# Edge rows fetched by strip and half a ring at a time, instead of by third of a group

## What is computed

```
xn = layernorm(x)
m  = xn[src] @ Wg[:256] + edge_attr @ Wg[256:]          # 106250 edges
g  = segment_sum(m * deg^-0.5[dst], dst) + h_bias
a  = gelu((q @ (LN(k)^T LN(v) / N) + xn) @ w1 + b1) @ w2 + b2 + xn    # linear attention, 8 heads
x  = x + g + a
x  = x + layernorm(top-2 experts FFN(layernorm(x)) + layernorm(x))    # one routing for all rows
```

## Time and profile before

| | before |
|---|---|
| median of 3 runs | 1550.7 us |
| profiled execution | 1550.73 us |
| its span | 1548.9 us |
| edge phase (first to last matmul of L849) | about 64 to 1141 us |
| GpSimd: gathers of L527, busy | 814.9 us of 831 gathers |
| TensorE busy (share of the span) | 1126.2 us (73%) |
| DMA queue 1 (SyncE) | 149305 packets, 159.30 MB |
| DMA queue 0 (GpSimd) | 39888 packets, 108.97 MB |

### The profile page before, as it was taken

One profiled execution on the slowest core, in us unless ns is written; L12 is line 12 of the kernel. 1 busy time (PEld: TensorE's weight loads), 2 busy tenths in 40 slices (PEclk: granted clock), 3 DMA queues, 4 the chain that ended last, 5 costly groups with the idle time before them and its releaser, 6 DMA issues. The chain is left out here.

```text
span 1548.9 us, 22938 instructions
## 1 busy us (share of the span) xinstructions
PE 1126.2 (73%) x7317; PEld 815.4 (53%) x7317; DVE 682.0 (44%) x1616; ACT 485.8 (31%) x1006; POOL 977.3 (63%) x1005
## 2 busy tenths in 40 slices
PE   0167787877677777777677677667566499999997
PEld 0035454544444544444454444444333199999997
DVE  6144555455545553232222222231017656666665
ACT  5411111111111110221111112111027667767764
POOL 5577777777777777777777776767734224333332
PEclk9998888888878887788778878878779889999998
DMA  9976767776767675978888887889634100000001
GB/s 271 292 247 209 232 202 224 217 233 194 218 207 226 208 215 182 250 219 244 237 236 242 247 227 223 242 242 302 189 86 127 47 20 23 20 23 23 20 22 32
DMA packets 195653, 275.73 MB, mean 178 GB/s; under 512 B 20021, under 2 KB 166577, under 8 KB 194318
## 3 DMA queue, kind: packets, MB, share of 16 engines
q1 hardware_dynamic: 149305, 159.30, 35.0%
q0 software_dynamic: 39888, 108.97, 23.6%
q10 hardware_dynamic: 6375, 6.40, 1.2%
HBM read 255.38 MB, written 19.23 MB: 177 GB/s over the span
## 5 line engine op out<-in xcount | busy, mean ns | idle before, releaser
L527 POOL DMA_INDIRECT ring<-xn_table,src_sb x831 | 814.9, 981 | 281.0 <-issue 245.4
L849 PE MATMUL bank<-ring,s 128*32 128x512 f32 x1662 | 267.7, 725 | 282.0 <-DMA ring<-xn_table,src_sb 225.4
L863 PE MATMUL bank<-fl_t,wg 128*128 128x128 f32 x1120 | 221.0, 379 | 19.0 <-ACT fl_t L600 18.9
L849 PEld LDWEIGHTS bank<-ring,s 128*32 128x32 f32 x1662 | 39.8, 116 | 352.4 <-issue 272.7
L863 PEld LDWEIGHTS bank<-fl_t,wg 128*128 128x128 f32 x1120 | 211.9, 291 | 20.7 <-ACT fl_t L600 20.7
L1200 DVE TENSOR_TENSOR acc<-acc,bank 128x96 f32 x277 | 70.6, 255 | 342.5 <-PE bank L863 225.5
L1205 DVE TENSOR_TENSOR xt_lo<-bank,xt_hi 128x250 fp32r<-128x250 f32 (+1 forms) x75 | 37.8, 505 | 260.2 <-ACT xt_hi L600 260.2
L589 POOL TENSOR_TENSOR rx<-vex,half 125x2 f32<-125x2 f32 x25 | 17.7, 708 | 181.9 <-DVE nmx L1451 181.9
L1068 PE MATMUL bank<-xf_hi,fw_hi 128*128 128x256 f32 x400 | 113.5, 284 | 9.4 <-DVE fw_lo L1477 7.2
L1430 DVE TENSOR_TENSOR h_lo<-h,h_hi 128x512 fp32r<-128x512 f32 x100 | 95.8, 968 | 49.6 <-ACT h_hi L600 49.6
L1079 PE MATMUL bank<-fw_hi,h_hi 128*125 128x256 f32 x400 | 113.7, 284 | 0.0
(11 more groups left out here) (207 smaller groups left out, 2155.4 us busy)
## 6 DMA issues: line engine op xcount, KB each, us to landing
ring<-edges SPq DMA_DIRECT2D x207, 512.0 KB
ring<-xn_table,src_sb POOLq DMA_INDIRECT x831, 3.9
xnr<-xn_table SPq DMA_DIRECT2D x50, 125.0 KB
xnr<-xn_table SPq DMA_DIRECT2D x25, 250.0 KB
xch<-x SPq DMA_DIRECT2D x25, 250.0 KB
base_rows<-xch ACTq DMA_DIRECT2D x25, 250.0 KB
out<-res SPq DMA_DIRECT2D x25, 250.0 KB
acc<-x SPq DMA_DIRECT2D x5, 1120.0 KB
```

Source lines behind the costliest of these rows:

```text
L527: pool.indirect_dma_start(out=to, out_offset=None, in_=table, in_offset=bass.IndirectOffsetOnAxis(ap=index, axis=0),).then_inc(done, 16)
L849: mm = pe.matmul(ps_seg[t % 2][j * W:(j + 1) * W, :], lhsT=s32[:, t % 3, j * TS + i, :].bitcast(F32), rhs=ring[:, u, j, :], start=i == 0, ...
L863: mm = pe.matmul(ps_y[:, o * P:(o + 1) * P], lhsT=wg[:, c, o * P:(o + 1) * P], rhs=fl_t[:, c, :], start=c == 0, stop=c == 3)
```

## The change

`edge_load` now takes a group t instead of a third. It fetches strip by strip: for strip j one DMA reads, per partition, three consecutive rows (3 KB in one piece in DRAM) and writes them to three ring slots, the half of the ring that the group uses (slots 0 to 2 for even t, 3 to 5 for odd t). A group has four DMAs of 384 KB instead of three of 512 KB. Only two semaphores count them, one per half, and TensorE waits once per group, in its first third, for all four. SyncE issues the loads of group t+1 in its third 3t, ahead of that third's other loads, and waits before them until group t-1 is done, which is third 3t - 1 (`s_seg` at 3t).

```diff
-        def loaded(q):
-
-            return 16 * (q // RS + 1)
+        def loaded(t):
+
+            return 16 * ST * (t // 2 + 1) if t < NG - 1 else 16 * ST * (t // 2) + 16 * TS
...
-            def edge_load(q):
-
-                t, i = divmod(q, TS)
-                u = q % RS
-                wait_past(sp, s_seg, q - RS + 1)
+            def edge_load(t):
+
+                wait_past(sp, s_seg, TS * (t - 1))
+                u = TS * (t % 2)
                 if t < NG - 1:
-                    rows = edges[t * GE:(t + 1) * GE, :].rearrange("(j p k) d -> p j k d", p=P, k=TS)[:, :, i, :]
-                    sp.dma_start(ring[:, u, :, D:2 * D], rows).then_inc(s_e[u], 16)
+                    for j in range(ST):
+                        a = (t * ST + j) * SE
+                        rows = edges[a:a + SE, :].rearrange("(p k) d -> p k d", k=TS)
+                        sp.dma_start(ring[:, u:u + TS, j, D:2 * D], rows).then_inc(s_e[t % 2], 16)
                 else:
-                    rows = edges[FULL + i:E:TS, :]
-                    sp.dma_start(ring[0:rows.shape[0], u, 0, D:2 * D], rows).then_inc(s_e[u], 16)
+                    for k in range(TS):
+                        rows = edges[FULL + k:E:TS, :]
+                        sp.dma_start(ring[0:rows.shape[0], u + k, 0, D:2 * D], rows).then_inc(s_e[t % 2], 16)
...
-            for q in range(3):
-                edge_load(q)
+            edge_load(0)
...
             for q in range(NQ):
-                if q >= 3:
-                    edge_load(q)
+                if q % TS == 0 and q // TS + 1 < NG:
+                    edge_load(q // TS + 1)
                 if kv_at(q, 0) is not None:
                     kv_load(kv_at(q, 0))
...
-                pe.wait_ge(s_e[u], loaded(q))
+                if i == 0:
+                    pe.wait_ge(s_e[t % 2], loaded(t))
                 pe.wait_ge(s_gat[u], arrived(q))
```

## The result

The changed kernel takes 1810.81 us (median of 4 runs, 1787 to 1818), the kernel before 1550.45 in the same comparison. The ratio is 1.1623, 95% interval 1.1509 to 1.1738: slower by 16%. Ratio and interval leave out one of the four runs (1817.69 us), which is counted as one in a slower state. The profiled execution took 1808.09 us, its span 1806.2, 257.3 more than before. The forecast of 1743 had the sign and the closed loop; it was 68 us short.

What follows compares the result with a forecast made beforehand. GpSimd's gathers were taken to bound the edge phase, except the mix stretch, where TensorE also waits for SyncE's queue. 1550.7 us plus 176 for the mix stretch and 17 for the kv stretch gave 1743.7, stated as 1743, range 1625 to 1850.

Steps and rivals of the forecast that it cites:

- What bounds the kernel now: Edge phase: GpSimd's gathers, 15.4 us a group; in the mix stretch a 16.67 us period with TensorE waiting for SyncE's queue.
- Fewer or larger transfers: Edge loads: 207 pieces of 512 KB become 276 of 384 KB, with 3 KB runs in DRAM; priced at nothing.
- The order moved: SyncE's queue: mix load issued late behind 1536 KB; mix period 23.7 us against 16.67, 176 us over 25 groups.
- T: Mix stretch: time from the end of strip sums 3t-1 until the mix load has landed, put at 14.7 us.
- The first two parts: Terms of T: 1.7 us fixed, plus 7.1 us for 1536 KB of edge rows at 222 GB/s.
- the third part: Term of T: the 500 KB mix load, 4.0 us alone, 5.9 us beside the gathers.
- the harder rival: Mix and kv stretches both at their long bounds, ACT's store sharing engines with the burst: up to 1946 us; chance 0.07.
- The prediction's other estimate: Mix stretch: five engines at 27 GiB/s less gathers, 9.0 us for edge and mix rows; T = 10.7, 75 us more.
- The kv stretch: 34 groups in 17 pairs: late kv loads make a pair 30.4 us against GpSimd's 30.7; 17 us for jitter.
- The rival that loads overtake the pieces: Queue: mix load overtakes edge pieces or lands by 7.7 us, so no difference, 1551 us; chance 0.04.
- the faster one: Mix stretch: 3 KB pieces help, mix load not held up, GpSimd's 15.4 us binds; 32 us less, 1519; chance 0.07.
- The milder rival: Mix load goes at the edge pieces' pace: T = 11.1, period 20.1 us, 85 us more, 1636; chance 0.22.

Runs made afterwards that it cites:

- e1: Changed kernel with each group's kv loads and mix load issued ahead of the next group's edge pieces; 1697.88 us beside 1682.37, ratio 1.0090.
- e2: Kernel before, pieces still by third, but issued at the change's place and behind its wait; 1910.79 us beside 1682.37, ratio 1.1353.
- e9: Changed kernel with ACT's store issued two thirds later, behind the mix transposes; ratio to the kernel before 1.1279.
- e8: Changed kernel with mix loads and ACT's store each cut into partitions 0 to 111 and 112 to 124; ratio to the kernel before 1.0985.
- e3: Changed kernel with each mix load cut into partitions 0 to 111 and 112 to 124; ratio to the kernel before 1.1243.
- c_after: Changed kernel run again without edits, as reference on a chip of the experiments; 1941.96 us beside 1681.69, ratio 1.1554.
- e6: Changed kernel with two of four strip pieces ahead of the mix load and two behind, in the mix stretch alone; 1903.35 us, ratio to the kernel before 1.1314.
- e7: Changed kernel with the mix load behind the same wait but ahead of all four edge pieces; 1845.41 us, ratio to the kernel before 1.0984.
- e11: Changed kernel with mix load behind the same wait, ahead of edge pieces and cut at partition 112, ACT's store two thirds later; 1741.17 us beside 1694.43, ratio 1.0287.

## Why the prediction was right, and which term was too small

What bounds the kernel now, right: with the loads ahead (e1) the kernel is back within 0.9%, so the edge pieces themselves were no bound.

Fewer or larger transfers cost nothing, right in the mix stretch, by e1 and e2; in the kv stretch e2 leaves 20 us open between the shape and the wait for the whole group, where the loads come late. The packets show that 3 KB runs weren't even moved as longer ones. The rule that the prediction cites there is on whole transfers; that it would favour 3 KB pieces inside one was my reading of it.

The order moved, right: a closed loop from `s_seg` over SyncE's wait, the burst and the mix load to TensorE, 25 times. The part beside T, 9.0 us, measured 8.8 in the period shown.

T was the term that was mis-sized: 17.5 in the period shown (17.4 by the mean period less 8.8), not 14.7. The first two parts held as far as can be told: the last edge piece is issued near 914.3, and if it lands after the median of 6.3 us the pieces are in by 920.6, 8.8 us after the clock's start, as 1.7 + 7.1; no row shows this landing itself. Then the third part, the mix load, took the remaining 8.7 us where I had 5.9. I had scaled the lone store's time by 327/222, for the gathers. Two things were left out. One: ACT's store of 250 KB starts within 0.2 us of the edge burst; I had put it in the harder rival and not in the sum, and e9 and e8 price it at 1.2 and 1.5 us of wait. Two: the full engines don't move the 327 GB/s of the slice that I picked, but 241 to 365 from slice to slice. In e8 nearly everything is spread over all engines, and the edge pieces, mix load, store and eight gathers, 3.39 MB in 12.4 us, still average 273 GB/s. And one sign was misread: the share of 0.59 at 858 to 860 says nothing of the mix load issued at 858.79, for ahead of that issue, from 856 to 858, it is 0.56. That the load uses few engines is shown only by the tail after the change and by e3.

The prediction's other estimate, T = 10.7, was worked out from the 27 GiB/s an engine that the Trainium skill gives, page "DMA: Bandwidth & Descriptors", section "Specifications". It fell farther short of the measured 17.5.

An account that fits the sizes, worked out from the runs: take five engines for a load or store of 125 rows and sixteen for the rest. Until the mix load lands, the busiest engines carry 98 KB of edge pieces ahead, 102 of the mix load, 51 of the store and 66 of the eight gathers that GpSimd issues before it stops. With T as the mean period less 8.8, less the fixed 1.7, that is 317 KB in 15.6 us for c_after, 268 in 14.3 for e6, 266 in 14.4 for e9, 247 in 13.5 for e3, 219 in 11.8 for e7 and 212 in 12.4 for e8: 17 to 20 GB/s an engine in all six. It foretold the waits of e8 and e11 before they ran, and e9's at twice its size. In e11 the busiest engines have 33 KB of the load and, by four gathers, as much of those, and these 66 KB land in 5.1 us, less 1.7, which is 19. It is still only an estimate: from c_after to e8 the busiest engines lose 105 KB, 5.5 us at 19 GB/s, and T falls by 3.2. So it gives the size of T and overrates most single steps, as e3, e6, e7 and e9 all gave less than expected. What sets that remainder is open, and the gathers' share was argued and not tried by itself. In the 24 mix periods the change cost 228 us where the forecast's 7.0 each make 168; these 60 us are nearly all of what it fell short.

The kv stretch: 17 us forecast, 24.6 between the first and last kv transposes. The pair's pattern was right, the waits (5.9 and 6.6 in even groups, 3.5 in an odd one) of the order of the 8 and 1.6 worked out, the odd one twice as long. Another 7.6 us were lost ahead of the first kv transpose, which I had at nothing, and 4.8 came back before the first mix one.

The rival that loads overtake the pieces fell, with the faster one: T never came near 7.7 in the changed kernel. The milder rival (T = 11.1, load spread evenly over the engines) was refuted by T = 17.5 and by the tail from 923 to 929; even with load and store cut (e8) T is 14.1, the period of 22.9 less 8.8. GpSimd's wait was foretold as 200 us and is 285 (263 in the mix stretch), TensorE's ahead of the mix transposes 285 and is 359; both carry the same error in T.

## What to carry to other kernels

When loads are merged and moved, look at what else is issued behind them on the same queue: a short load that was ten microseconds early stood behind 1536 KB and a wait for the newest result, and that closed a loop through three engines. Put what is needed next ahead of what is needed later (e1 took back all but 0.9% with that alone). Price a transfer by all that moves beside it until it lands, stores of other queues and the few engines that a shape may leave it included, not by the rate of one slice of the trace. And try such causes together as well as one by one: the cut and the later store gave 2.0 and 1.2 us alone, and with the burst out of the way 8 us together.

## What was not expected

A load of 125 rows leaves a tail: six microseconds with all compute engines idle at DMA shares of 0.46 to 0.18, gone when it is cut at row 112. Longer runs in DRAM left the packets at about 1 KB (150409 for 159.31 MB). And the kernel before took 1550 us in the first comparison and 1682 to 1694 on the chips of the experiments, while the change cost 260 us in two of the three places, by chance.
